# Attention output and rows of maxima turned by VectorE's 32x32 block transposes instead of TensorE, with a new order of all pieces

## What is computed

```python
# layer 0, for each sequence (layer 1: RMS norm, interleaved rope, swiglu instead of gelu)
h = _ln(x) * (1.0 + s1) + sh1
qkv = h @ qkv_w.T + qkv_b                    # 16 heads of 16 channels
q = q * cos + _rotate_half(q) * sin          # k the same
scores = einsum('bqhd,bkhd->bhqk', q, k) / sqrt(16)
o = einsum('bhqk,bkhd->bqhd', softmax(scores), v).reshape(B, L, C)
x = x + (o @ proj_w.T + proj_b) * g1
h2 = _ln(x) * (1.0 + s2) + sh2
x = x + (gelu(h2 @ fc1_w.T + fc1_b) @ fc2_w.T + fc2_b) * g2
```

## Time and profile before

| | value |
|---|---|
| median of 3 runs | 792.26 us |
| span of the profiled execution | 789.7 us (its own time with what lies around the span isn't given) |
| PE busy | 748.3 us, 95%, 4800 matmuls |
| DVE busy | 626.9 us, 79%, 1097 instructions |
| ACT busy | 477.6 us, 60% |
| POOL busy | 291.4 us, 37% |
| mean granted TensorE clock | 0.987 of 2.4 GHz |

### The profile page before, as it was taken

The page is one execution under the profiler, slowest core; times in us unless marked ns, Lnnn a source line. Parts: engine busy times, 40 slices in busy tenths (PEclk is TensorE's granted clock), DMA queues, the critical chain, the costliest instruction groups (busy, mean ns, idle before and its releaser), DMA issues.

```text
span 789.7 us, 13682 instructions
## 1 busy us (share of the span) xinstructions
PE 748.3 (95%) x4800; PEld 465.6 (59%) x4800; DVE 626.9 (79%) x1097; ACT 477.6 (60%) x761; POOL 291.4 (37%) x267
## 2 busy tenths in 40 slices
PE   5989889999999999999999999999999999999697
PEld 4543334475546754566546654668547685677497
DVE  3988998888779987898888899878878879755354
ACT  2127774787467765778568867665556646566232
POOL 1502204443544435452464444322344132423243
PEclk9979999999999999999999999999999999999899
DMA  8548340231131411232121333241031412000000
GB/s 322 148 140 257 87 148 25 83 95 42 41 95 28 108 42 42 67 90 59 37 73 42 95 108 97 66 108 42 27 94 28 109 41 64 6 1 1 28 1 27
DMA packets 31603, 59.45 MB, mean 75 GB/s; under 512 B 6064, under 2 KB 10800, under 8 KB 31280
## 3 DMA queue, kind: packets, MB, share of 16 engines
q1 hardware_dynamic: 31536, 58.58, 25.5%
HBM read 39.42 MB, written 18.87 MB: 74 GB/s over the span
## 4 chain that ended last, share of the span: by engine, by line
PE 74%; DVE 7%; issue 4%; POOL 3%; ACT 3%; DMA 2%; SPq 2%; ACTq 0%; DVEq 0%; POOLq 0%
PE ring L1039 19%; PE ps_o L969 12%; PE ps_b L1056 12%; PE ring L939 9%; PE ring L954 8%; PE ring L903 5%; DVE top L1235 4%; PE ring L1009 3%; PE ring L916 2%; ACT pr L1491 2%; PE ring L980 2%; SPq L847 1%; POOL sines L1605 1%; PE ring L885 1%; DMA qt<-top_t 1%
## 5 line engine op out<-in xcount | busy, mean ns | idle before, releaser
L1235 DVE TENSOR_REDUCE top<-ring 128x2 f32<-128x1024 f32 x256 | 307.3, 1220 | 47.1 <-PE ring L954 44.6
L1491 ACT ACTIVATE pr<-ring 128x1024 f32<-128x1024 f32 x256 | 255.7, 1023 | 80.7 <-PE ring L939 74.1
L1648 POOL TENSOR_TENSOR act_l<-mlp,act_h 128x256 fp32r<-128x256 f32 x128 | 102.9, 804 | 237.4 <-DVE act_h L1317 237.4
L969 PE MATMUL ps_o<-pr,va 128*17 128x512 f32 x1024 | 132.2, 597 | 0.1
L939 PE MATMUL ring<-qt,kt 49*128 49x512 f32 x512 | 113.4, 462 | 6.7 <-DMA qt<-top_t 2.8
L954 PE MATMUL ring<-kt,qt 48*128 48x512 f32 x512 | 112.4, 456 | 7.3 <-DVE top L1235 3.8
L1528 ACT ACTIVATE mlp<-ring,col 128x256 f32<-128x256 f32 x128 | 60.4, 472 | 84.4 <-PE ring L1039 71.5
L939 PEld LDWEIGHTS ring<-qt,kt 49*128 49x128 f32 x512 | 46.4, 184 | 86.3 <-issue 40.3
L1039 PE MATMUL ring<-hh,wl 128*128 128x256 f32 x384 | 84.1, 301 | 2.8 <-DVE hh L1292 1.2
L1303 DVE SCALAR_TENSOR_TENSOR mlp<-mlp 128x256 f32<-128x256 f32 x128 | 58.4, 457 | 35.4 <-ACT mlp L1535 25.0
L954 PEld LDWEIGHTS ring<-kt,qt 48*128 48x128 f32 x512 | 48.1, 187 | 60.2 <-issue 19.4
(11 more groups left out here) (89 smaller groups left out, 1022.9 us busy)
## 6 DMA issues: line engine op xcount, KB each, us to landing
scratch<-high SPq DMA_DIRECT2D x16, 512.0 KB, 3.8
scratch<-low SPq DMA_DIRECT2D x16, 512.0 KB, 4.2
qt<-scratch SPq DMA_DIRECT2D x64, 128.0 KB, 2.6
kt<-scratch SPq DMA_DIRECT2D x64, 128.0 KB, 2.7
mlp<-in_w_split SPq DMA_DIRECT2D x20, 256.0 KB, 3.0
qt<-scratch SPq DMA_DIRECT2D x64, 64.0 KB, 2.6
kt<-scratch SPq DMA_DIRECT2D x64, 64.0 KB, 2.7
xs<-in_x SPq DMA_DIRECT2D x4, 512.0 KB, 4.6
```

The costliest lines, as they stand in the source:

```text
L969: last = nc.tensor.matmul(ps_o[32 * h:32 * h + HD + 1, :], va[:, u % 2, t, QUAD * g + h, :], pr[:, slot, :], start=(t == 0), stop=(t == T ...
L1235: nc.vector.tensor_reduce(top[:, n % 2, 0:4 * T].rearrange("p (e c) -> p e c", e=2)[:, :, c], pair[:, :, :], AX_X, ALU.max, negate=True).t ...
L1491: nc.scalar.activation(pr[:, at % NP:at % NP + 2, :], pair[:, :, :], ACT.Exp, scale=SCALE).then_inc(free, 1)
L1648: nc.gpsimd.tensor_tensor(act_l[:, at % 2, :], src, act_h[:, at % 2, :].bitcast(F32), ALU.subtract).then_inc(act_l_in, 1)
```

## The change

- **Maxima.** `top` and `top_t` become [128, 2, 32] in float32r. VectorE transposes `top` in 32x32 blocks itself (`top_turn`, a piece of VectorE now). TensorE's transpose and ScalarE's copy are gone. The rows then lie in four groups of 16 partitions with 32 positions each, and SyncE issues four DMAs for a quad, not two, each of 16 rows of 128 B.
- **Output of a quad.** VectorE transposes `ps_o` in 32x32 blocks to `lanes` (`to_lanes`), which frees `ps_o`; takes the reciprocal of 16 denominators in each partition, and multiplies 16 x 16 values into `scaled` (`output`). ScalarE's copy and TensorE's four transposes are gone.
- **Channels of two quads.** After every second quad VectorE transposes `scaled` (128x512) in blocks to `oc` (`back`), from which `project` reads. TensorE's `o_turn` and ScalarE's `channels` are gone, and `hf` no longer takes the attention output. The rows of the projection weights are reordered on the host to the channel order of `oc`.
- **Order.** The tables of ticks are replaced by `ORDER`, one place for each piece of all units, 2168 pieces in place of 2240. Among others: the first unit's q and k come before its v, the two first chunks of `split_w` come before the first `peaks`, ScalarE's `split_w` 0 to 2 come before the first `modulated`, and the load `trig`, second of the twelve `load` pieces before, now stands behind `t1`, `ada1`, `row`, `ada2`, `x1`, `t2`, `grow` and three weight chunks.

```diff
-    return pieces + [(tick, engine, "output", n) for tick, engine in zip(at["output"], ("act", "pe", "dve"))]
+    pieces += [("dve", "lanes", n), ("dve", "output", n)]
+    if n % 2:
+        pieces.append(("dve", "back", n // NQ, n % NQ // 2))
...
+ORDER = {
...
+        ("sp", "load"): (28, 86, 2, 32, 72, 1, 70, 57, 179, 681, 160, 485),
+        ("sp", "load_w"): (31, 33, 68, 136, 139, 177, 198, 216, 301, 302, 334, 370, 1235, 1236, 1237, 1371, 1373,
...
+        ("act", "modulated"): (16, 17, 335, 336, 82, 83, 612, 613, 276, 277, 878, 879, 555, 556, 1157, 1158, 821, 823,
...
+        ("act", "split_w"): (6, 7, 8, 112, 123, 144, 220, 271, 272, 287, 324, 328, 1364, 1365, 1375, 1391, 1392, 1421,
...
 def program():
 
-    return [p[1:] for p in sorted(ticked(), key=lambda p: p[0])]
+    at = {kind: iter(places) for kind, places in ORDER.items()}
+    return [piece for _, piece in sorted((next(at[piece[:2]]), piece) for piece in all_pieces())]
...
                 def top_row(n):
 
-                    sp.wait_ge(*emptied("top", n))
-                    for e in range(2):
-                        sp.dma_start(qt[STACK * e + SHIFT:STACK * e + SHIFT + 1, n % NSLOT, :, :].bitcast(F32),
-                                     top_t[8 * e:8 * e + 8, n % 2, :].bitcast(F32)).then_inc(top_in[n % 2], 16)
+                    sp.wait_ge(top_turned, n + 1)
+                    for a in range(P // BLOCK):
+                        sp.dma_start(qt[SHIFT:SHIFT + STACK + 1:STACK, n % NSLOT, :, :].rearrange(
+                            "e h (t a q) -> e (h t) a q", t=T, a=P // BLOCK)[:, :, a, :].bitcast(F32),
+                                     top_t[a * BLOCK:a * BLOCK + 4 * T, n % 2, :].bitcast(F32)
+                                     ).then_inc(top_in[n % 2], 16)
...
-                        pe.wait_ge(*emptied("o", u, KC - 1))
+                        pe.wait_ge(back_in, KC * (u + 1))
...
+                def top_turn(n):
...
+                    ve.wait_ge(*emptied("peaks", n, T * QUAD // 2 - 1))
+                    nc.vector.transpose(top_t[:, n % 2, :].bitcast(F32), top[:, n % 2, :].bitcast(F32)).then_inc(top_turned, 1)
+
+                def to_lanes(n):
+
+                    ve.wait_ge(pv_done, T * (n + 1))
...
+                    nc.vector.transpose(lanes[:, :, :].rearrange("p j d -> p (j d)"), ps_o[:, :]).then_inc(o_free, 1)
+
                 def output(n):
 
...
+                    ve.wait_ge(o_free, n + 1)
+                    step(nc.vector.reciprocal(rden[:, :], lanes[:, :, HD]))
                     settled()
...
+                    nc.vector.tensor_tensor(scaled[:, :, half * HD:(half + 1) * HD], lanes[:, :, 0:HD],
+                                            rden[:, :].unsqueeze(2).to_broadcast([P, L // BLOCK, HD]), ALU.mult
+                                            ).then_inc(scaled_in, 1)
+
+                def back(u, k):
+
+                    ve.wait_ge(scaled_in, NQ * u + 2 * k + 2)
...
+                    nc.vector.transpose(oc[:, k, :], scaled[:, :, :].rearrange("p j d -> p (j d)")).then_inc(back_in, 1)
```

More of the change, by code:

```diff
@@ L24 @@
 SHIFT = 3 * HD
+BLOCK = 32
 HALVES = 2
@@ L200, in top_pieces @@
-def top_pieces(n):
-    return [("pe", "top", n), ("act", "top", n), ("sp", "top", n)]
-def quad_pieces(n):
-    at = QUAD_AT[QUAD_KIND[n // NQ]][n % NQ]
-    more = n + 1 < NALL
-    pieces = []
-    for m in range(T * QUAD // 2):
-        pieces.append((at["scores"][m], None, "scores", n, m))
-    for m in range(T * QUAD // 2):
-        pieces.append((at["peaks"][m], None, "peaks", n, m))
-    pieces += [(tick, *piece) for tick, piece in zip(at["top"], top_pieces(n))]
-    pieces += [(at["values"][t], "pe", "values", n, t) for t in range(T)]
-    if n + 2 < NALL:
-        pieces += [(at["fill"], "sp", "fill", n + 2)]
-    return pieces + [(tick, engine, "output", n) for tick, engine in zip(at["output"], ("act", "pe", "dve"))]
@@ L430, with quad_pieces @@
+    pieces += [("pe", "net_2", part) for part in range(NET_PARTS)] + [("dve", "net_2")]
+    return pieces + [("sp", "load", name) for name in LOADS]
+LOADS = ("row", "trig", "ada1", "ada2", "grow", "t1", "t2", "x1", "wf0", "wf1", "x2", "x3")
 LAST = NU - 1
 TURNED = ("h1", "h2", "h2_rest")
+def quad_pieces(n):
+    pieces = [(None, "scores", n, m) for m in range(T * QUAD // 2)]
+    pieces += [(None, "peaks", n, m) for m in range(T * QUAD // 2)]
+    pieces += [("dve", "top", n), ("sp", "top", n)]
+    pieces += [("pe", "values", n, t) for t in range(T)]
+    if n + 2 < NALL:
+        pieces += [("sp", "fill", n + 2)]
+    pieces += [("dve", "lanes", n), ("dve", "output", n)]
+    if n % 2:
+        pieces.append(("dve", "back", n // NQ, n % NQ // 2))
+    return pieces
@@ L455, in post_pieces @@
         if u < LAST:
-            pieces.append((at["proj"][2 * half + 1], "pool", "residual", u, "proj", half))
-    pieces += norm_pieces(u, 1, at["norm"])
+            pieces.append(("pool", "residual", u, "proj", half))
+    pieces += norm_pieces(u, 1)
     if u == LAST:
-        pieces += norm_pieces(u, 2, at["norm2"])
-        pieces += [(at["bias"][2 * i + half], "pool", "bias", u, name, half) for i, name in enumerate(("proj", "fc2"))
-                   for half in range(2)]
-    for n, ticks in enumerate([at["split"]] + ([at["split2"]] if u == LAST else [])):
+        pieces += norm_pieces(u, 2)
+        pieces += [("pool", "bias", u, name, half) for name in ("proj", "fc2") for half in range(2)]
@@ L463, in post_pieces @@
+    for n in range(1, 2 + (u == LAST)):
         for k in range(KC):
-            pieces += [(ticks[k], "dve", "split_h", u, n + 1, k), (ticks[2 + k], "pool", "split_h", u, n + 1, k)]
+            pieces += [("dve", "split_h", u, n, k), ("pool", "split_h", u, n, k)]
     follow = (("act", "hidden"), ("dve", "cube"), ("act", "tanh"), ("dve", "hidden"), ("pool", "hidden"))
@@ L487, in pre_pieces @@
     for pair in range(2):
-        pieces += [(tick, *piece) for tick, piece in zip(at["rope"][pair], rope_pieces(u, pair))]
+        pieces += rope_pieces(u, pair)
     for t in range(T):
-        pieces += [(at["v"][t], "pe", "v", u, t), (at["take_v"][t], "dve", "take_v", u, t)]
+        pieces += [("pe", "v", u, t), ("dve", "take_v", u, t)]
     return pieces
-def split_pieces(chunks, at):
-    pieces = []
-    for i, c in enumerate(chunks):
-        pieces += [(at["load"][i], "sp", "load_w", c), (at["act"][i], "act", "split_w", c),
-                   (at["dve"][i], "dve", "split_w", c)]
-    return pieces
@@ L918, in v @@
                     last.then_inc(full, 1)
-                def top_turn(n):
-                    bank, full, _, _ = place("top", n)
-                    for wait in room("top", n):
-                        pe.wait_ge(*wait)
-                    pe.wait_ge(*emptied("peaks", n, T * QUAD // 2 - 1))
-                    nc.tensor.transpose(bank[:, 0:P], top[:, n % 2, :], eye[:, :]).then_inc(full, 1)
                 def scores(n, m):
```

530 lines of the change are left out of this document (135 added, 395 removed), and 77 rows, old and new, of the table ORDER.

## The result

The changed kernel takes 810.41 us (median of 4 runs, 808.44 to 814.24); the kernel before took 792.9 us beside it. The ratio is 1.0218, 95% interval 1.0175 to 1.0261: 17.3 us slower, where 13.6 us faster was forecast. Further down every "+x us" is the measured ratio to the kernel before, less one, times 793 us, so that runs on different chips can stand together. Each ratio's interval is 2 to 5 us wide to either side, and a difference of two kernels is less certain than either. Traces are of one execution: the changed kernel's is its slowest of four (814.24 us at a mean granted clock of 0.962; the others had 0.968 to 0.972).

A forecast was written before the change was run, and what follows sets the result against it. TensorE was taken to bound the middle, VectorE close behind. Middle -13.1, tail -2.5 and head +2.0 sum to -13.6 us: span 789.7 becomes 776.1, the median 779, own range 772 to 788, overall range 763 to 801.

The forecast's parts named there:

- TensorE is the bound, VectorE close behind: Middle, 100 to 700 us: TensorE busy 586.4 of 600 us and the bound, VectorE next with 503.0.
- The sizes: VectorE's transposes in the middle: 42 at 0.60 us, 25.2 us, and 27 of the maxima at 0.16, 4.3 us.
- Rival D: VectorE's float32 transposes go at half pace, 1.20 us for 512 columns: 807 us, slower; chance 0.12.
- The estimate that stood beside the sum: From 311 ns for 128 bf16 columns, 0.71 us per 512-column VectorE transpose: 5 us more VectorE work in the middle.
- Product: Reciprocal and product on VectorE, same element count, now from SBUF: 0.05 us off each pair, 1.4 us.
- What it makes of the middle: With VectorE needing 531.1 us at a held share of 0.905, the middle takes 586.9 us, a gain of 13.1.
- rival B: VectorE is no bound, the new order holds it above 0.92, the middle gives all 25.3 us: 767; chance 0.22.
- Waits that have nothing to do with the turned pieces: Named way to be wrong: the new order adds or removes such waits, which the sum can't see; no size.
- Transfers of the maxima: SyncE's four DMAs per quad, not two, issue 1.3 us more; the shorter round gives it back: nothing taken.
- Head: `modulated` waits for loads to 17.4 us, first reduction at 42 to 46: +2.0 us taken, ends -3 and +7.
- Tail: From last `ps_o` copy to projection, 4.09 us becomes 2.0; with the quad before, -2.5 us in all.

The follow-up runs named there:

- the cuts: Changed kernel with GpSimd's sines, low parts, gate product and residual sum cut in pieces: 797.27 us; with the `act_l` subtractions cut too, 793.39 us.
- e18_head_whole: Changed kernel, no GpSimd cuts, with the earlier kernel's 80 first pieces, `split_w` 0 to 2 and `load_w` 1, 2 behind `peaks(0, 3)`: 808.29 us, ratio 1.0179.

## Why the prediction was wrong

**TensorE is the bound, VectorE close behind.** Right for the kernel before. In the changed one it no longer holds: TensorE's share of the last chain is 45%, VectorE's 33%, and a microsecond of TensorE is worth about half of one.

**The sizes.** TensorE's matmuls are 4576, as said. VectorE's transposes were mis-sized: 0.706 and 0.700 us for 512 columns, not 0.60, and 0.203 for 32, not 0.16; over the 42 and 27 of the middle that is 42 x 0.10 + 27 x 0.04 = 5.4 us. Rival D (1.2 us) is out; its 807 us lies nearest to the 810 by luck. The estimate that stood beside the sum from the Trainium skill, page "VectorE: DVE Perf Modes", section "The three transpose paths", 0.71 us, was the right one, though it was made from its figure for bf16.

**Product.** Wrong: "stay with the same count of elements, now read from SBUF" was priced as 0.05 us saved. Reading from SBUF is what lets GpSimd hold it, +0.215 us each, 6.9 us in 32; where it isn't held it takes 0.425 us as before, so that the saving wasn't there either. I looked at the element count and not at where the operands lie.

**What it makes of the middle.** This is the step that gave the wrong sign. I took a share of VectorE that an in-order engine can hold, 0.905, and turned the rest into time: 13.1 us gained. From the first to the last reduction it is 16.6 us lost. VectorE held 0.93 of the middle, as in my rival B, and the middle was slower all the same: over the whole kernel 44 us of VectorE's busy time more than before was waiting for GpSimd inside the operations, which a busy share counts as work. By the measured prices, 27.8 us less of TensorE's work (192 x 0.12 + 32 x 0.15) at 0.51 is 14 us gained, and 40.3 + 6.9 us more of VectorE's at 0.3 is 14 us lost: the exchange of engines would come out even, and the 17 us that remain are what the cuts gave back. This is an estimate and not shown: each slope is uncertain by about half its size or more, they are of the changed kernel, and in the old order the same exchange costs 39 us with hardly any held time. What the runs do show is that in the new order the cuts undo the loss.

**Waits that have nothing to do with the turned pieces.** I named this as the way to be wrong and gave it no price. ORDER places the norm's products beside GpSimd's sines and low part, and where TensorE needs a held product it stands, and the granted clock falls during the stop: at 331.9, 427.5 and 519.6 us, together 20.4 us at half clock that weren't there before and that are gone with the sines and the low part cut. Over the whole profiled run, stops included, granted clock times span is 30.9 us short of full speed after (812.4 x 0.038) and was 10.3 before, but 9 of these 20.6 us lie in the first 100 us. The rule of the page "SBUF — State Buffer" of the Trainium skill was there to be laid over the new order, two lists against each other, before any run.

**Transfers of the maxima.** I took nothing, by three waits of 2.3 us in all. Issuing four takes 0.8 us more than two, not 1.3, and the smaller pieces of 128 B land no later: the scores start 1.16 to 1.18 us after the last issue where they wait for the row, and 1.25 to 1.26 with pieces of 512 B. Few and short waits were no slack: in 11 of 32 quads of the kernel before the scores start as soon as the row has landed, and in the old order the same step costs 8 us. In the new order four transfers bind in 7 quads only, so "nothing" is nearly right there; no run takes the two away.

**Head.** Mechanism right, size of the delay too small: modulation at 20.55 us (forecast about 17.4), first reduction at 52.6 (forecast 42 to 46), 10.2 us late. In time it is worth 3 by `e18_head_whole`, within the noise of nothing and of the +2.0 that I took.

**Tail.** Right. From the start of `lanes` to the projection it takes 2.26 us where it took 4.09:

```profile
758.17 0.72 DVE L1063 STREAM_TRANSPOSE lanes<-ps_o 128x512 f32<-128x512 f32 x1 [5.93 <-PE ps_o L800]
758.92 0.25 DVE L1069 RECIPROCAL rden<-lanes 128x16 f32<-128x16 f32 x1
...
760.43 3.29 PE L818 MATMUL ring<-wf,oc 128*128 128x256 f32 x14 [1.44 <-DVE oc L1084]
```

From the last reduction to the end it is 77.9 us, it was 82.0.

**What stays open.** Why the output's turning alone costs 23 us in the old order, with little held time: TensorE waits more for reductions (10.0 us in 21 waits), for `oc` ahead of the projection (5.7) and for the transfer of the maxima (8.4 in 8, where it was 2.8), which fits VectorE's queue being late by the added operations, but no run takes that apart. And whether the half clock by itself, without the waits that bring it, is worth what it seems.

## What to carry to other kernels

When a change moves work to VectorE or reorders it, lay its SBUF-only products, copies and tensor_scalar operations against GpSimd's large operations, because each collision can cost a whole GpSimd operation; cutting those operations gave 14 us back where TensorE waits for what is held, and cost 3 where little is. A busy share says neither that the engine works nor that its relief pays: take a known amount off each engine, or add it, and read the slope. And a small wait at a hand-over is not slack: count how often the receiver starts as soon as the hand-over lands, and take that number times the added time.

## What the runs showed of the hardware

- VectorE's 32x32 block transposes of float32 take 0.706 us from PSUM and 0.700 from SBUF for 128x512, 0.203 for 128x32. Those of 128x512 take the same beside a busy GpSimd as alone.
- GpSimd holds whole VectorE operations by kind of operand: six of 128x256 take 14.5 us in place of 2.3 (tensor_scalar), 14.5 in place of 1.9 (copy) and 14.9 in place of 2.7 (two SBUF inputs), 2.7 in both cases with an input in PSUM.
- Four GpSimd products of 128x256 take 3.4 us where one of 128x1024 takes 2.6; the cut pays only by what it lets through.
- A transfer of 16 rows of 128 B into two partitions costs SyncE 495 ns to issue and one of 8 rows of 512 B into one partition 650 ns, but eight of 8 rows of 128 B 632 ns each: issuing time didn't go by bytes.
- In a stop of TensorE of 4.01 us its granted clock fell to 1.2 GHz, 1.9 us after the stop began, and stayed there for 6.8 us, 4.7 of them with TensorE at work again.
